# Residual and final-state transposes off TensorE: VectorE 32x32 blocks and a transfer through HBM, in a four-layer graph kernel on one core

## The reference

```
x = layernorm(x + L0(x))   # two gated aggregations over adj, gated self loop, relu
x = layernorm(x + L1(x))   # normalised aggregation, linear, batchnorm, relu, linear, batchnorm
x = layernorm(x + L2(x))   # graph attention: scores, mask, softmax over nodes, attention @ (x W)
x = layernorm(x + L3(x))   # two graph convolutions, then LSTMs over windows of 1, 2, 3, 4 nodes
```

## Time and profile before

| | us |
|---|---|
| median of 3 executions | 638.23 (637.72 to 639.11) |
| span of the profiled execution, first to last instruction | 636.4 |
| TensorE busy in it | 621.6 |
| VectorE, ScalarE, GpSimd busy | 474.8, 433.8, 167.4 |

### The profile page before, as it was taken

How to read it: one execution, slowest core, us unless ns; L and a number is a source line. 1 busy time by engine, 2 the same in 40 slices (tenths; PEclk the granted TensorE clock), 3 DMA queues, 4 the chain that set the end, 5 groups by cost and what they waited for, 6 DMA issues and landing times.

```text
span 636.4 us, 9580 instructions
## 1 busy us (share of the span) xinstructions
PE 621.6 (98%) x2768; PEld 440.9 (69%) x2768; DVE 474.8 (75%) x1623; ACT 433.8 (68%) x995; POOL 167.4 (26%) x228
## 2 busy tenths in 40 slices
PE   9999999999999999999999999999999999999994
PEld 6756656447975687578658757865885687577794
DVE  4999999876847767866887787688768767465656
ACT  3667767966947766795677577557847766546774
POOL 1464551005233002304503240341143032103211
PEclk9999999999999999999999999999999999999998
DMA  8424000000000000000000000000000000000000
GB/s 337 142 115 166 1 1 1 1 0 2 2 1 1 0 2 0 2 2 33 2 0 2 34 1 2 33 2 1 1 33 2 2 28 6 1 1 33 2 35 33
DMA packets 4372, 16.84 MB, mean 26 GB/s; under 512 B 480, under 2 KB 480, under 8 KB 4192
## 3 DMA queue, kind: packets, MB, share of 16 engines
q1 hardware_dynamic: 4320, 16.23, 6.6%
HBM read 12.03 MB, written 4.19 MB: 26 GB/s over the span
## 4 chain that ended last, share of the span: by engine, by line
PE 76%; DVE 3%; ACT 2%; issue 1%; POOL 0%; POOLq 0%; ACTq 0%; DVEq 0%
PE QQ L831 26%; PE QQ L843 15%; PE PA L814 4%; PE PA L786 4%; PE PB L805 2%; PE PB L796 2%; PE PB L667 2%; PE PA L667 2%; PE PA L767 2%; PE PB L767 2%; PE QQ L865 1%; PE PB L884 1%; PE PB L746 1%; PE PA L746 1%; PE QQ L875 1%
## 5 line engine op out<-in xcount | busy, mean ns | idle before, releaser
L1200 ACT ACTIVATE raw<-QQ,BL 128x256 f32<-128x256 f32 (+2 forms) x279 | 150.1, 558 | 75.1 <-PE QQ L843 37.7
L831 PE MATMUL QQ<-HT,WT 128*128 128x256 f32 (+2 forms) x558 | 183.9, 474 | 1.1 <-ACT raw L1200 0.6
L446 POOL TENSOR_TENSOR RSD<-VAR,pw 128x4 f32<-128x4 f32 (+1 forms) x43 | 61.8, 1438 | 381.7 <-DVE VAR L1422 381.7
L831 PEld LDWEIGHTS QQ<-HT,WT 128*128 128x128 f32 x558 | 103.5, 190 | 59.2 <-issue 28.3
L843 PE MATMUL QQ<-HB,WT 128*128 128x256 f32 (+2 forms) x336 | 100.2, 441 | 0.4 <-DVE HB L1708 0.2
L843 PEld LDWEIGHTS QQ<-HB,WT 128*128 128x128 f32 x336 | 61.2, 190 | 29.3 <-issue 13.4
L1236 ACT ACTIVATE raw<-raw 128x256 f32<-128x256 f32 (+4 forms) x79 | 37.1, 470 | 25.9 <-DVE raw L1690 19.7
L1680 DVE SCALAR_TENSOR_TENSOR raw<-raw 128x256 f32<-128x256 f32 (+2 forms) x60 | 32.5, 542 | 20.2 <-ACT raw L1200 19.6
L1708 DVE SCALAR_TENSOR_TENSOR HB<-raw 128x256 f32<-128x256 f32 (+4 forms) x42 | 20.1, 478 | 23.5 <-ACT raw L1236 23.5
L1042 ACT ACTIVATE X<-Z,OFF,RSD 128x128 f32<-128x128 f32 x80 | 31.8, 482 | 2.0 <-POOL OFF L452 2.0
L512 POOL TENSOR_SCALAR X<-four,MEAN,RSD 128x128 f32<-128x128 f32 x64 | 30.7, 494 | 1.6
(11 more groups left out here) (249 smaller groups left out, 1177.5 us busy)
## 6 DMA issues: line engine op xcount, KB each, us to landing
four<-in_x SPq DMA_DIRECT2D x8, 512.0 KB, 4.0
raw<-in_xt SPq DMA_DIRECT2D x8, 512.0 KB, 6.5
out<-four SPq DMA_DIRECT2D x7, 512.0 KB, 2.6
WT<-in_lstm SPq DMA_DIRECT2D x1, 2048.0 KB, 8.0
later<-in_later SPq DMA_DIRECT2D x1, 725.5 KB, 10.3
AD<-in_adj SPq DMA_DIRECT2D x2, 256.0 KB, 4.8
out<-four SPq DMA_DIRECT2D x2, 256.0 KB, 2.0
early<-in_early SPq DMA_DIRECT2D x1, 275.0 KB, 4.5
```

The costliest lines, as they stand in the source:

```text
L446: pool.tensor_tensor(RSD[kk][:, ts], VAR[kk][:, ts], pw[:, ts], ALU.pow).then_inc(ln[k]["rstd"], some)
L831: mm = pe.matmul(steps_view(Q[q], k), WT[:, 0, (p - 1) * 4 + q, :], ht_view(par, k), start=True, stop=(s == 0))
L1200: act.activation(TG[q][:, at:n], Q[q][:, at:n], ACT.Tanh, scale=0.5 if q == G else 0.25, bias=BL[:, p - 1, q:q + 1]).then_inc(g_ok, 1)
```

## The change

Both groups of 8 transposes leave TensorE. In their place VectorE transposes the 32x32 blocks of a 128x1024 tensor in one instruction (`y_blocks`, `t_blocks`). SP writes that to a scratch tensor in HBM and, when the write has landed, reads it back with four DMAs, one for each destination quarter of 32 partitions, which puts the blocks in their places. The residual sum of L2's input moves to GpSimd (`y_sum`, from SBUF, two instructions) and, with its statistics and transposes, a turn ahead. The final sum `t_sum` becomes four instructions of 256 columns and stands behind `a_hidden` with `t_stats`. The end of the attention of the last two graphs of a group (`a_mix` of graph 3, `a_project_mix` of 2 and 3, their sums and normalisation) and `a_spread0` of the convolution move into or later within the next turn. `a_dots` is cut in two halves, the first between the states of LSTM steps 0 and 1. `a_rows` writes PSUM tensor PB in place of PA. ScalarE takes gates I and G of step 0 at the end of the turn before. The last group's final transposes (`t_turn_half`) stay on TensorE.

In the diff below stand, in this order: SP, GpSimd, TensorE, ScalarE and VectorE. `t_through` on SP is like `y_through`, with `t_blk`, `t_put`, `t_got`, and is issued first in a turn.

```diff
+        YD, YF = late[:, 2, 0:COLS], late[:, 2, COLS:2 * COLS]
+        TD, TF, JUNK = (O2T[:, k * COLS:(k + 1) * COLS] for k in range(3))
...
+        turn_y = nc.dram_tensor("turn_y", (GROUPS, P, COLS), F32, kind="Internal").ap()
+        turn_t = nc.dram_tensor("turn_t", (GROUPS, P, COLS), F32, kind="Internal").ap()
...
+        def quad_rows(buf, q):
+            return buf[q * QUAD:(q + 1) * QUAD, :].rearrange("p (q n) -> p q n", q=P // QUAD)
+        def quad_source(scratch, q):
+            return scratch.rearrange("(a p) (q n) -> q p a n", p=QUAD, q=P // QUAD)[q]
...
+            def y_through(g):
+                sp.wait_ge(y_blk, g - 1)
+                sp.dma_start(turn_y[g], YD).then_inc(y_put, 16)
+                sp.wait_ge(y_put, 16 * (g - 1))
+                reach(sp, z1_ok, NC * (g - 2))
+                for q in range(P // QUAD):
+                    sp.dma_start(quad_rows(YF, q), quad_source(turn_y[g], q)).then_inc(y_got, 16)
...
+            def y_sum(g):
+                pool.wait_ge(y_got, 64 * (g - 1))
+                reach(pool, dots_ok, 2 * TILES * (g - 2))
+                pool.wait_ge(ln[1]["out"], TILES * g)
+                for c in range(NC):
+                    pool.tensor_tensor(Z[:].rearrange("p (b c q i) -> p c b q i", c=NC, b=GB, i=QUAD)[:, c],
+                                       YF.rearrange("p (q b c i) -> p c b q i", c=NC, b=GB, i=QUAD)[:, c],
+                                       X1[:, g, :].rearrange("p (c b q i) -> p c b q i", c=NC, b=GB, i=QUAD)[:, c],
+                                       ALU.add).then_inc(z1_ok, 1)
...
             def slot(s, par, A, B, L, T):
+                if s > 2 and B:
+                    rstd(2, 1, s - 1, 1)
+                    scale2(s - 1, 1)
                 if A:
-                    rstd(1, 0, s)
                     scaled(s + 2)
+                if A and s + 1 < GROUPS:
+                    y_sum(s + 1)
                 if T:
                     tail(s - 3, 1 - par)
                 if A:
-                    for h in range(2):
-                        rstd(2, 1, s, h)
-                        scale2(s, h)
+                    if s + 1 < GROUPS:
+                        rstd(1, 0, s + 1)
+                    rstd(2, 1, s, 0)
+                    scale2(s, 0)
...
+            def a_rest(g):
+                if g > 1:
+                    a_project_mix(g, (2,))
+                    a_mix(g, (3,))
+                a_spread0(g, (0, 1), 0)
+                if g > 1:
+                    a_project_mix(g, (3,))
...
                 x(0)
-                a_residual(s) if A else None
                 x(1)
-                t_turn(s - 3, 1 - par) if T else None
-                a_spread0(s - 1, (0, 1)) if B else None
+                a_rest(s - 1)
                 x(2)
-                a_spread0(s - 1, (2, 3)) if B else None
+                a_rows(s)
                 x(3)
                 h(3)
-                a_rows(s) if A else None
-                a_weigh0(s - 1) if B else None
+                a_spread0(s - 1, (2, 3), 1)
+                a_weigh0(s - 1, 0)
                 x(4)
+                a_weigh0(s - 1, 1)
                 x(5)
...
                 x(9)
-                if A:
-                    a_mix(s, (0, 1, 2))
-                    a_project_mix(s, (0, 1))
+                a_mix(s, (0, 1))
+                a_project_mix(s, (0,))
                 h(9)
                 x(10)
-                if A:
-                    a_mix(s, (3,))
-                    a_project_mix(s, (2,))
+                a_project_mix(s, (1,))
+                a_mix(s, (2,))
                 h(10)
-                a_project_mix(s, (3,)) if A else None
...
-                cell(0)
+                gates(0, None if s == 2 else (O,))
+                state(0)
                 cell(1)
+                a_mixed(s - 1, (3,)) if s > 2 else None
+                a_spread(s - 1, 0)
+                norm_apply(1, 0, Z, s, X2, 0) if A else None
                 cell(2)
...
+                gates(10)
+                lstm_gates(s - 1, 0, (I, G))
+                state(10)
...
+            def t_blocks(g):
+                dve.wait_ge(h_ok, NSTEP * (g + 1))
+                reach(dve, t_put, 16 * g)
+                dve.transpose(TD.rearrange("p (q c b i) -> p b c q i", c=NC, b=GB, i=QUAD),
+                              by_batch(HT[:, g % 2]).rearrange("p b (c q i) -> p b c q i", c=NC, i=QUAD)).then_inc(t_blk, 1)
             def t_sum(g):
-                dve.wait_ge(ht_ps, g + 1)
+                dve.wait_ge(t_got, 64 * (g + 1))
                 reach(dve, ln[3]["out"], TILES * g)
-                dve.scalar_tensor_tensor(out=ZF[:], in0=PB[:], scalar=0.5, in1=X1[:, g, :], op0=ALU.mult,
-                                         op1=ALU.add).then_inc(zf_ok, 1)
+                for q in range(P // QUAD):
+                    dve.scalar_tensor_tensor(out=z[:, :, q], in0=quads(TF)[:, :, q], scalar=0.5, in1=x3[:, :, q], op0=ALU.mult,
+                                             op1=ALU.add).then_inc(zf_ok, 1)
+            def y_blocks(g):
+                dve.wait_ge(yt_ok, g + 1)
+                reach(dve, y_put, 16 * (g - 2))
+                dve.transpose(YD.rearrange("p (q t i) -> p t q i", t=TILES, i=QUAD),
+                              O2T[:, g * COLS:(g + 1) * COLS].rearrange("p (t q i) -> p t q i", t=TILES, i=QUAD)).then_inc(y_blk, 1)
```

More of the change, by code:

```diff
@@ L417, in _, with t_through, slot @@
             sp.dma_start(WT[:], lstm_w).then_inc(lstm_in, 16)
-            for g in range(GROUPS - 1):
-                sp.wait_ge(ln[3]["out"], TILES * (g + 1))
-                sp.dma_start(out[g], OUT[:, g % 2]).then_inc(sent[g % 2], 16)
+            def y_through(g):
[5 more added lines that the diff above has]
+                    sp.dma_start(quad_rows(YF, q), quad_source(turn_y[g], q)).then_inc(y_got, 16)
+            def t_through(g):
+                sp.wait_ge(t_blk, g + 1)
+                sp.dma_start(turn_t[g], TD).then_inc(t_put, 16)
+                sp.wait_ge(t_put, 16 * (g + 1))
+                reach(sp, zf_ok, P // QUAD * g)
+                for q in range(P // QUAD):
+                    sp.dma_start(quad_rows(TF, q), quad_source(turn_t[g], q)).then_inc(t_got, 16)
+            def slot(s, par, A, B, L, T):
+                g = s - 3
+                if T and g < LAST:
+                    t_through(g)
+                if A and s + 1 < GROUPS:
+                    y_through(s + 1)
+                if T and g < LAST:
+                    sp.wait_ge(ln[3]["out"], TILES * (g + 1))
+                    sp.dma_start(out[g], OUT[:, g % 2]).then_inc(sent[g % 2], 16)
+            y_through(2)
+            slots(slot)
             half = TILES // 2 * P
@@ L445, in rstd @@
                 pool.wait_ge(ln[k]["var"], n)
+                pool.wait_ge(ln[1]["out"], TILES * g) if k == 1 and g > 1 else None
                 pool.tensor_tensor(RSD[kk][:, ts], VAR[kk][:, ts], pw[:, ts], ALU.pow).then_inc(ln[k]["rstd"], some)
@@ L549, in _ @@
             scale2(0, 1)
+            y_sum(2)
             rstd(2, 2, 1, 0)
@@ L671, in _ @@
                 output1(i, h)
[L674 to L681, removed]
             def a_preload(g, h):
@@ L876, in lane_h @@
                               start=False, stop=True).then_inc(v.ps, 1)
-            def t_turn(g, par):
-                pe.wait_ge(h_ok, NSTEP * (g + 1))
-                pe.wait_ge(z2_ok, upto(g + 3) * TILES)
-                reach(pe, y1_ok, 2 * upto(g + 2)) if g + 3 >= GROUPS else None
-                for c, b in ORDER:
-                    mm = pe.transpose(tile(PB, c, b), by_batch(HT[:, par])[:, b, c * P:(c + 1) * P], ident[:])
-                mm.then_inc(ht_ps, 1)
             def t_turn_half(par, c):
@@ L924, in slot @@
                     x(1)
-                    t_turn(s - 3, 1 - par)
-                    a_spread0(LAST, (0, 1), 0)
+                    a_rest(LAST)
                     x(2)
@@ L1185, in lstm_gates @@
                 j = NSTEP * g + k
-                for q in gates_of(k):
+                for q in some or gates_of(k):
                     act.wait_ge(g_ps, NGATE * g + GATE_AT[k, q] + 1)
@@ L1238, in slot, with gates @@
             def slot(s, par, A, B, L, T):
-                def gates(k):
-                    lstm_gates(s - 2, k) if L else None
+                def gates(k, some=None):
+                    lstm_gates(s - 2, k, some) if L else None
                 def state(k):
@@ L1811, in slot @@
                     cell(0)
-                    t_sum(s - 3)
+                    t_blocks(s - 3)
                     cell(1)
@@ L1883, in _ @@
             a_norm2(0, 0)
+            y_blocks(2)
             a_sum2(0, (2,))
```

109 lines of the change are left out of this document (50 added, 59 removed).

## The result

| | before | after |
|---|---|---|
| median, us | 638.12 (637.72 to 639.11, 4 executions) | 659.56 (657.96 to 661.54, 4 executions) |
| span of the profiled execution | 636.4 | 656.2 |

The changed kernel is slower: 1.034 times the time before, 95% interval 1.0326 to 1.0354. The forecast was 653 us, range 640 to 660.

The account below looks back on a forecast made before the run. TensorE's list was taken to set the pace. Full turns +11.0, turn 2 -1.3, turn 8 +3.0, turn 9 +1.4 and prologue +0.6 made +14.7 on the 636.4 span: 651.1, median 653 us, range 640 to 660.

Parts of the forecast that it names:

- step 7: Turns 3 to 7: `t_sum` and `t_stats` before cell 7 delay `h(8)`; TensorE stands about 1.9 us a turn.
- steps 0 and 1: Turns 3 to 7: dots before cell 1 and late cell 10 delay `x(2)`; 1.8 us standing, lower end 1.0.
- Score rows: `a_rows` right behind `x(2)` waits for VectorE's sums, dots and scaling: 0.35 us, between nothing and 0.8.
- Full turn: Turns 3 to 7: 55.7 + 1.9 + 1.8 + 0.35 = 59.7 us, 2.2 above 57.5; five of them +11.0.
- Transposes: VectorE's block transposes between state 3 and cell 4: 1.2 us for y, up to 2.0 the other; cost taken 0.
- Turn 8: No `a_turn_e` there, so the 3.1 us of sum and statistics come in full: +3.0 us.
- Turn 9: `t_turn`'s 0.95 goes, `t_blocks` takes `t_sum`'s place, `t_sum` goes among the lanes: +1.4 us, between 0 and 2.5.
- TensorE's busy time: Sign in the profile after: about 12 us less, from `a_residual` and `t_turn` leaving TensorE.
- first rival: Only step 7 stands, steps 0 and 1 covered or nearly so: 642 to 647, or 639; chance 0.2.
- The second: Rival that the promise holds, the time taken off TensorE comes back: faster, 626 to 636 us; chance 0.12.
- third rival: Port: GpSimd's `y_sum` holds up VectorE's cells, or a transpose is far over 2 us: 659 to 665; chance 0.1.
- The fourth: Rival that HBM data comes late, over 18 us, so `t_sum` holds VectorE at cell 7: beyond 659; chance 0.03.

Follow-up runs that it names:

- Experiment 1: Changed kernel with `t_sum` moved behind cell 5 and `t_stats` between cell 6 and `a_hidden`: 646.43 us, 1.0118 times before.
- Experiment 3: Changed kernel with the first 8 of each turn's 16 dots replaced by one memset: 652.93 us, 1.0226 times before.
- experiment 6: Changed kernel with VectorE's sums of cell 10 moved ahead of the norm 2 statistics (`a_norm2`): 654.85 us, 1.0264 times before.
- experiment 2: Changed kernel with all 16 dots together behind state 1, none before cell 1: 664.3 us, 1.0398 times before.
- Experiment 4: Changed kernel with turn 9's transposes back on TensorE and its sum and statistics in their old places: 655.19 us, 1.0268 times before.
- experiment 10: Changed kernel with GpSimd doing its residual sum twice, the first two instructions without a reader: 661.03 us, 1.0374 times before.
- experiment 8: Kernel of experiment 7 with the second half of the next group's `a_stats1` moved ahead of cell 9: 636.9 us, 0.9988 times before.
- experiment 7: Changed kernel with the edits of experiments 1, 4 and 6 together: 638.63 us, 1.0014 times before.
- experiment 9: Kernel of experiment 8 with ScalarE's last mixed copy before step 1's tanh and group 2's first eight dots in the prologue: 635.18 us, 0.9962 times before.

## Why the prediction was right

The direction and the mechanism held: TensorE was freed, and the same two links, step 7 and steps 0 and 1, made it wait. 653 was 6.6 too low. In the profiled spans (656.2 for 651.1) the gap is 5.1, and 3.7 of it is in turns 8 and 9, not in the full turns; the other 1.5 is that the median execution was longer than the profiled one. The measured time is 0.44 inside the end of the range, and one of the four executions lies beyond it. Point by point:

- **Step 7, 1.9 us a turn:** the distance from `x(7)` to `h(8)` grew by 1.5 to 1.8 (in turns with the smaller value `x(7)` itself waited 0.15 more). `t_sum` took 1.41 for 1.45 and `t_stats` 1.65 for 1.64. Experiment 1 took 13.1 away, where 5 x 1.9 + 3.1 = 12.6 had been counted. That the two are so near is partly luck: by the spans it is 7.5 for 9.5 in the full turns, and 4.3 for 3.1 in turn 8, where 1.4 is the clock's.
- **Steps 0 and 1, 1.8 us:** cell 1 at +8.56 for +8.2, and from there 2.23 to `x(2)` for 2.24, so +10.79 for +10.4. The link that was short is cell 10, at +2.25 for +1.7. Experiments 3 and 6 show both parents, the dots and the late cell 10. The sign given, a gap of 1.8 right before `x(2)`, did not come: most of the 2.16 stands inside `x(1)` and is ended by ScalarE, a wait that the forecast did not name.
- **Score rows, 0.35:** they begin 2.92 after `x(2)`, whose six products take 2.58: 0.34.
- **Full turn 59.7:** 59.80 to 59.87 in four, 60.21 in turn 7, where the second wait inside `x(1)` is 0.58 in place of 0.21; 12.1 together for 11.0.
- **Turn 2, -1.3:** -1.1. **Prologue, +0.6:** +0.66. **Transposes:** 2.03 and 1.20, at the bounds taken, and covered. **Transfers:** 12.9 us for both, for 12 to 15.
- **Turn 8, +3.0:** +4.4, the term that was mis-sized for lack of a mechanism. The stand came as forecast (3.21), but behind it TensorE ran `h(8)` at the lower clock, 1.4 more than before. Even this has no fixed size: behind the same stand turn 8 took 55.7 to 57.1 in the profiles of the changed kernel and of experiments 2, 3, 4, 6 and 10.
- **Turn 9, +1.4:** +3.7, outside its own bounds of 0 to 2.5. This is the step with the largest error: "`t_sum` goes among the lanes" was priced like work under cover, while in turn 9 there is none. Experiment 4 takes 2.8 of it back.
- **TensorE's busy time 12 us less:** only 2.4 less, this sign was wrong. A restart after a wait is itself counted busy: `x(0)` and `x(1)` are 5.16 of products and count as 2.74 + 1.98 + 0.97 = 5.69 in turn 4, and the slow `h(8)` adds 1.5. In experiment 8, with most waits gone, a turn of 56.67 has 56.02 busy, nearer to the 55.7 that was worked out. I have not followed the rest.
- **Two slips on paper:** in the first rival, "639 if turn 9 and the prologue cost nothing" is the span; the median would be 640.4. And `y_sum` ran at +38 to +42 of the turn, not at +34 to +37, so it met cell 6 and state 6.

Of the rivals, the first (only step 7 stands) was wrong, since `x(2)` stood too. The second, that the promise holds, is what experiments 7 to 9 approach: once the three places are mended the kernel is 21 to 24 us faster than the changed one, yet of the promised 11.9 us against the kernel before only 2.5 to 3 are left at best, in experiment 9. The 659.56 lies in the third rival's band, but not by its mechanism: the sum does hold VectorE, by 1.2 us in three turns, but in the changed kernel that is covered. The fourth, late data, did not occur.

Two things stay open. The longer executions of the changed kernel go with a lower mean clock, but only one was profiled, so behind which stands it fell in the others is not shown. And the 0.6 at `x(2)` that experiments 8 and 9 leave is probably the dots still between state 0 and cell 1; this is argued from the order of work, as moving them a turn ahead was not tried.

## What to carry to other kernels

Taking work off the engine that sets the pace buys nothing if the same edit puts work of another engine inside the pace setter's dependency loop. Before moving it, list for every loop how much filler stands against its way round, and put the new instructions where the second engine is idle or where nothing waits: here the same 3 us of work cost 11 to 13 us over the run, or next to nothing, by their place alone. Look hardest at the turns that lack a filler, the first and the last ones, for there nothing is covered.

## What the runs showed that I had not expected

- **The clock after a stand.** After stands of 1.2 to 1.7 us TensorE went on at a granted clock of 1.00. After 3.2 us it went on at 0.56, and eight products took 3.25 us for 1.73; the five other profiles with this stand show 0.50 to 0.74. Between them both occur. In turn 2 stands of 2.06 to 2.19 us left it at 1.00 in seven profiles, but in experiment 10 a stand of 2.06 at the same place was followed by 0.63 (first row), and in its turn 4 one of 2.50 by 0.65:

```profile
197.70:202.20 4.50, 4.45 (x8) 1.84 (x9) 2.56 (x18) 2.29 (x6) 0.00 (x0) 0.63 0.00 0
...
352.50:355.00 2.50, 0.08 (x1) 0.00 (x0) 1.95 (x10) 0.42 (x1) 0.00 (x0) 1.00 0.00 0
355.00:358.10 3.10, 3.02 (x9) 2.50 (x10) 2.60 (x11) 1.42 (x3) 2.12 (x3) 0.65 0.00 0
```

So a stand has a second price, and its length alone does not tell it: the same 2.06 us were followed by a full clock in experiment 6 and by 1.6 us of loss in experiment 10. What decides between the two is not shown here.

- **Half a us from who starts first.** In experiments 7 to 9 the stand before `h(8)` is gone, so nothing swallows what GpSimd's sum holds up on VectorE. In turn 5 of experiment 8 the sum began first, at 395.68, and the last instruction of cell 6 took 1.40. In turn 4 this instruction began 0.08 ahead of the sum (339.45 against 339.53) and took its usual 0.51. The timelines of VectorE in turn 4 and turn 5:

```profile
339.45 0.51 DVE L1744 SCALAR_TENSOR_TENSOR raw<-raw 128x340 f32<-128x340 f32 x1
...
396.14 1.40 DVE L1744 SCALAR_TENSOR_TENSOR raw<-raw 128x340 f32<-128x340 f32 x1
```

Turn 4 took 56.67 and turn 5 57.16, and only in turn 5 did `x(7)` wait for state 6. It is the same in all three experiments: of turns 3 to 6, those in which cell 6 was held are 0.5 longer than those in which it was not. So the third rival's mechanism costs nothing in the changed kernel and 0.5 us in two or three turns of the mended ones. No edit tested this by itself.

- **The block transpose on VectorE.** 128x1024 float32 in blocks of 32x32 took 1.20 us for y, which is read in order, and 2.03 for the final state, which is read with a stride of four elements, as much as `a_hidden`'s strided write (2.02). The stride was not tested by itself. The way through HBM was as estimated: 8.5 us for y from the issue of the write to the sum.
